# A four-layer graph network: destination bins in steps of two slots, layer 0 sums by half turn, a bilinear update in ten blocks, spread padding rows

## The reference, cut to what matters

```
edge_index = jnp.stack([src, dst])
h = jnp.maximum(_layernorm(x, axis=-1), 0.0)
x = x + _L0_gnn_ref(h, node_vec1, src, dst, edge_attr_4, edge_attr_12, ...)
...
# inside layer 0
ns = jax.ops.segment_sum(mid_s, edge_dst, num_segments=N) * inv
nv = jax.ops.segment_sum(mid_v, edge_dst, num_segments=N) * inv
...
# inside layer 2: a0, a1 are the summed messages, xs, xv the nodes
u0 = jnp.einsum('nu,nv,uvw->nw', xs, a0, Wu_ss) * INV64 + jnp.einsum('nui,nvi,uvw->nw', xv, a1, Wu_vv) * (INV_SQRT3 * INV32)
u1 = jnp.einsum('nu,nvi,uvw->nwi', xs, a1, Wu_sv) * INV_SQRT2048 + jnp.einsum('nui,nv,uvw->nwi', xv, a0, Wu_vs) * INV_SQRT2048
u0 = u0 + xs @ Lu_s * INV8
u1 = u1 + jnp.einsum('nui,uw->nwi', xv, Lu_v) * INV_SQRT32
```

## Time and profile before

| | us |
|---|---|
| median of the runs | 14562.09 |
| all runs | 14611.6, 14537.42, 14562.09 |
| profiled execution, its own time | 14520.14 |
| its span | 14518.4 |
| granted TensorE clock, mean | 0.899 |

### The profile page before, as it was taken

The page is one execution under the profiler, slowest core; times in us unless marked ns, Lnnn a source line. Parts: engine busy times, 40 slices in busy tenths (PEclk is TensorE's granted clock), DMA queues, the critical chain, the costliest instruction groups (busy, mean ns, idle before and its releaser), DMA issues. The chain is left out here.

```text
span 14518.4 us, 298687 instructions
## 1 busy us (share of the span) xinstructions
PE 11751.5 (81%) x76172; PEld 8152.7 (56%) x76173; DVE 8626.0 (59%) x30542; ACT 5078.7 (35%) x15312; POOL 8651.1 (60%) x13301
## 2 busy tenths in 40 slices
PE   5445542888879999869996897799999999999998
PEld 1000000666645555336664797577777777777776
DVE  6455552899744443133332555677777777777776
ACT  0000000566512222111111000466666666666665
POOL 2777775676657676137775000466666666666665
PEclk9999999999979898655555898799999999999998
DMA  3101110333433335324448774000000000000001
GB/s 139 27 24 27 27 26 11 69 69 68 57 61 74 69 72 65 23 56 82 82 82 55 119 116 72 17 18 18 18 17 18 18 18 17 18 18 18 17 18 19
DMA packets 1123580, 666.64 MB, mean 46 GB/s; under 512 B 711710, under 2 KB 1045491, under 8 KB 1117786
## 3 DMA queue, kind: packets, MB, share of 16 engines
q0 software_dynamic: 257120, 382.51, 15.3%
q1 hardware_dynamic: 850410, 235.44, 9.4%
q10 hardware_dynamic: 15568, 43.25, 0.8%
HBM read 574.19 MB, written 86.47 MB: 46 GB/s over the span
## 5 line engine op out<-in xcount | busy, mean ns | idle before, releaser
L1099 POOL DMA_INDIRECT l2s_node_rows<-node_table,l2s_edge_rows x1216 | 1154.3, 949 | 871.0 <-DMA l2s_edge_rows<-rows_by_src 486.7
L1099 POOL DMA_INDIRECT l1s_node_rows<-node_table,l1s_edge_rows x1216 | 1256.4, 1033 | 648.5 <-issue 320.9
L1184 PE MATMUL l1s_p_outer<-l1s_edge_by_node,l1s_node_rows 128*32 128x64 f32 (+2 forms) x14592 | 1242.6, 274 | 130.6 <-DMA l1s_node_rows<-node_table,l1s_edge_rows 96.0
L448 PE MATMUL rank<-onehot,lower_h 128*128 128x418 f16 x812 | 429.6, 529 | 1021.9 <-DVE onehot L424 958.7
L1184 PE MATMUL l2s_p_outer<-l2s_edge_by_node,l2s_node_rows 128*64 128x40 f32 (+1 forms) x4864 | 1038.8, 345 | 247.9 <-DMA l2s_node_rows<-node_table,l2s_edge_rows 245.7
L731 POOL DMA_INDIRECT l_source_rows<-node_table,l_edge_rows x928 | 949.8, 1023 | 436.6 <-issue 271.7
L1184 PEld LDWEIGHTS l2s_p_outer<-l2s_edge_by_node,l2s_node_rows 128*64 128x64 f32 (+1 forms) x4864 | 839.0, 233 | 638.4 <-issue 412.3
L1184 PEld LDWEIGHTS l1s_p_outer<-l1s_edge_by_node,l1s_node_rows 128*32 128x32 f32 (+2 forms) x14592 | 768.5, 132 | 685.5 <-issue 509.9
L461 POOL DMA_INDIRECT rows_by_src<-row_s,pos_i x812 | 839.7, 1034 | 494.3 <-issue 494.3
L1855 POOL DMA_INDIRECT l_source_rows<-node_table,l_edge_rows x914 | 899.0, 984 | 318.6 <-issue 246.4
L1883 POOL TENSOR_TENSOR l_logits_kept<-l_logits,l_empty_row 128x8 f32<-128x8 f32 x456 | 432.0, 947 | 979.4 <-DVE l_logits L2164 979.4
(11 more groups left out here) (495 smaller groups left out, 32003.1 us busy)
## 6 DMA issues: line engine op xcount, KB each, us to landing
l_xv_by<-h_turned_l SPq DMA_DIRECT2D x300, 128.0 KB
l_source_rows<-node_table,l_edge_rows POOLq DMA_INDIRECT x1842
l_xs_by<-h_turned_l SPq DMA_DIRECT2D x100, 256.0 KB
l_a_by<-sums_turned_l SPq DMA_DIRECT2D x100, 256.0 KB
rows_by_src<-zero_rows ACTq DMA_DIRECT2D x23, 1024.0 KB
l1s_edge_rows<-rows_by_src SPq DMA_DIRECT2D x304, 76.0 KB
l2s_edge_rows<-rows_by_src SPq DMA_DIRECT2D x304, 76.0 KB
l1s_node_rows<-node_table,l1s_edge_rows POOLq DMA_INDIRECT x1216
```

Of the source, the lines that this page charges most:

```text
L448: nc.tensor.matmul(rank[:, b, 0:BINS], K["lower_h"][:, :], onehot[:, b, :], start=True, stop=False)
L1099: pool.indirect_dma_start(xg[q][:, s, :], None, table, bass.IndirectOffsetOnAxis(ap=pay[q][:, s, S_DST:S_DST + 1].bitcast(U32), axis=0)).t ...
L1184: ins = nc.tensor.matmul(p_o[rows, j % RING, col:col + n], xg[q][:, s, lhs], rhs(eh[q % RING][:, s, :, :]), start=True, stop=True, skip_gr ...
```

## The change

**Destination bins are padded to PAIR = 2 slots.** The bound on slots becomes 856 (214 quads, 216 turns of layer 0; 428 pairs, 432 turns of layer 3), and the sort's shift uses 2 x 128.

```
-QUADS_D = -(-((E + BINS_D * (QUAD * P - 1)) // (QUAD * P)) // 2) * 2
-SLOTS_D = QUADS_D * QUAD
+PAIR = 2
+SLOTS_D = -(-((E + BINS_D * (PAIR * P - 1)) // (PAIR * P)) // 2) * QUAD
+QUADS_D = SLOTS_D // QUAD
```

```
-                        pe.wait_ge(added, q + 1)
-                        for s in range(QUAD):
-                            ins = nc.tensor.matmul(p_sum[:, k, 0:MW], hot[k][:, s, :], msg[k][:, s, :], start=s == 0, stop=s == QUAD - 1)
-                        ins.then_inc(summed, 1)
+                        for h in range(HALVES):
+                            pe.wait_ge(added, HALVES * q + (h + 1))
+                            for s in range(PAIR):
+                                ins = nc.tensor.matmul(p_sum[:, h, 0:MW], hot[k][:, PAIR * h + s, :], msg[k][:, PAIR * h + s, :], start=s == 0, stop=s == PAIR - 1)
+                            ins.then_inc(summed, 1)
...
+                        for h in range(HALVES):
+                            dve.reg_load([bin_regs[h]], bins[0:1, bass.ds(q * QUAD + PAIR * h, 1)])
+                        for h in range(HALVES):
+                            b = dve.snap(bin_regs[h], min_val=0, max_val=NB - 1)
+                            dve.wait_ge(summed, HALVES * q + (h + 1))
+                            dve.wait_ge(added, HALVES * q + (h + 2))
+                            to = acc[:, bass.ds(b, 1), :].rearrange("p o f -> p (o f)")
+                            nc.vector.tensor_tensor(to, to, p_sum[:, h, 0:MW], ALU.add).then_inc(added, 1)
```

```
             @block.scalar
                 act.wait_ge(cleared, 1)
+                act.wait_ge(keys_in, 96)
                 n = 0
...
-                        act.dma_start(flat[:, at:at + w], zero[:, 0:w]).then_inc(zeros_written, 16)
+                        act.dma_start(flat[:, at:at + w], pad[:, :, :].rearrange("p r w -> p (r w)")[:, 0:w]).then_inc(zeros_written, 16)
```

```
+            on_pool = [len(members) == 3 and n == 2 for _, members, _ in groups for n, _ in enumerate(members)]
...
+                    eng.wait_ge(used, t * OPS + (OPS + used_for[m]))
+                    x, y = of(k)
+                    (nc.gpsimd if pool else nc.vector).tensor_tensor(prod[m % BUFS][:, :, :], x, free(y, [0, KB], [1, W]), ALU.mult).then_inc(made, 1)
...
+                                for j, w in enumerate(weights):
+                                    if kind == "v":
+                                        for i in range(3):
+                                            ins = mm(thirds[i], w, prod[(m0 + i) % BUFS][:, j, :], start=False, ...)
+                                    else:
+                                        ins = mm(halves[1 - j % 2], w, prod[m0 % BUFS][:, j, :], start=s_seen == 0, stop=stop)
```

```
+                    nc.vector.tensor_tensor(xb[:, 0:CS], turn[k][:, 0:CS], xb[:, 0:CS], ALU.add).then_inc(x_added, 1)
+                    nc.vector.tensor_tensor(xb[:, CS:D], turn[k][:, P:P + 3 * CV], xb[:, CS:D], ALU.add)
+                    dve.wait_ge(x_added, b + 2)
+                    nc.vector.tensor_tensor(xb[:, 0:CS], turn[k][:, CS:2 * CS], xb[:, 0:CS], ALU.add).then_inc(x_done, 1)
```

More of the change, by code:

```diff
@@ L321, in _ @@
                 nc.vector.memset(junk[:, 2, 0:1], 0.0).then_inc(keys_ready, 1)
+            @block.gpsimd
+            def _(pool):
+                nc.gpsimd.iota(spread_i[:, :], pattern=[[N // PAD_R, PAD_R]], base=0, channel_multiplier=0).then_inc(spread, 1)
             @block.tensor
@@ new lines, in stage_layer2, with upto @@
+            first_of = [sum(len(g[1]) for g in groups[:n]) for n in range(len(groups))]
+            def upto(m, pool):
+                return sum(1 for q in on_pool[:m] if q == pool)
+            had = [m - BUFS if m >= BUFS else max(x for x in range(OPS) if x % BUFS == m % BUFS) - OPS for m in range(OPS)]
+            freed = {}
+            for n, (_, members, _) in enumerate(groups):
+                for m in range(first_of[n], first_of[n] + len(members)):
+                    freed[m] = first_of[n] + len(members)
@@ L1551, in _ @@
                     v.after()
[L1552 to L1561 removed]
+                    dve.sem_inc(made_d, DVE_OPS)
@@ L1563, in _ @@
+                    with dve.Fori(0, T // 2) as tt:
+                        for k in range(2):
+                            products(dve, 2 * tt + k, k, False, made_d)
+                @block.gpsimd
+                def _(pool):
+                    pool.sem_inc(made_p, POOL_OPS)
+                    with pool.Fori(0, T // 2) as tt:
+                        for k in range(2):
+                            products(pool, 2 * tt + k, k, True, made_p)
                 @block.tensor
                 def _(pe):
-                    pe.sem_inc(used, STEPS)
```

302 lines of the change are left out of this document (188 added, 114 removed).

## The result

| | before | changed |
|---|---|---|
| median, us | 14586.85 (4 runs, 14537.42 to 14614.98) | 13978.19 (4 runs, 13953.48 to 14006.55) |
| profiled execution, its own time | 14520.14 | 14000.75 |
| its span | 14518.4 | 13999.0 |
| granted TensorE clock, mean | 0.899 | 0.880 |

The ratio is 0.9587, with a 95% interval from 0.9548 to 0.9626. The forecast was 13,945 in a range of 13,650 to 14,120. The medians lie 609 us apart, the profiled executions 519: the profiled execution before lies 67 us under its median, the changed one's 23 us above. The ratio is as the runs gave it; the quotient of the two medians is 0.9583.

A forecast was written before the change was run, and what follows sets the result against it. The bound was sought per stage: DVE in layer 0's loop, PE in the bilinear update. Terms -274 + 145 - 50 - 59 - 88 - 12 - 257 - 22 = -617 gave 13,903 us profiled, 13,945 median; range 13,650 to 14,120.

The forecast's parts named there:

- Fewer turns of layer 3: Layer 3's loop: 24 fewer turns of a pair at 11.43 us each, nothing inside a turn changed, -274 us.
- Layer 0: Layer 0's loop: 12 fewer turns, each remaining one with an uncovered extra register load and add, +145; tail -12 us.
- Order of the first transfers: Start: clearing writes wait for the destination keys, which arrive some 50 us sooner, by 35 to 40 us, -50 us.
- Spread padding: Node sums: last gathers run at the middles' rate; layer 1 -59, layer 2 -88, layer 0's last turns -12 us.
- Rival C: Node sums' tails: spreading the padding does nothing, +159, giving 14,104 us; chance 0.10.
- The update: Bilinear update in ten blocks: DVE's and POOL's products exclude each other and add to 67 us a block, -257 us.
- Rival B: Bilinear update: POOL's products lie beside DVE's, a block is DVE's 42.3 us, 248 less, 13,697 us; chance 0.13.
- PE side by side: Bilinear update: three 32-column or two 64-column matmuls at once, PE about 35 us a block, under 67.
- D: Bilinear update: side by side matmuls run serially at full clock, 88 us a block, +206, 14,151 us; chance 0.04.
- E: Bilinear update: serial matmuls with TensorE granted 0.50, 176 us a block, +1083, 15,028 us; chance 0.03.
- Stage back: Stage back: two buffers and half the pieces, at the copies' and adds' pace of 1.1 us, -22 us.

The follow-up runs named there:

- four-slot run: Destination bins padded to four slots again, with one sum and one add per layer 0 turn, against the changed kernel: 14044.84 us, ratio 0.9635 to the kernel before.
- zero-padding run: Changed kernel with padding rows all holding node 0 again: 14088.91 us against the unedited rerun's 13952.96, ratio 0.968 to the kernel before.
- Two runs: Changed kernel, clearing writes not waiting for the keys: 13933.71 us; kernel before with its tile of zeros set twice: 14475.1 us against 14545.99.
- its second: Profile of the changed kernel run again with no edit: median 13952.96 us, ratio 0.9612 to the kernel before.
- the ten with spread padding: Ten kernels with spread padding, run where the kernel before takes some 14,570 us; their layer 1 took 2172 to 2302 us.
- the PSUM run: Changed kernel with ACT copying DVE's factor into PSUM for 28 of its 30 products a block: 13700.42 us, ratio 0.9423 to the kernel before.

## Why the prediction was right, point by point

- **Fewer turns of layer 3 (-274).** Measured -286: 24 turns of 11.40, and 0.03 us less per turn. The four-slot run gives 269 by itself.
- **Layer 0 (+145, with -12 of the tail).** Measured +154.5 in all, +171 from the first add to the last and -17 after it. The mechanism was right: DVE closes the turn and both additions stand bare. Each was slightly under-sized. The second register load took 0.49 us (0.90 less 0.41) and not 0.41, and the turn 7.01 instead of 6.89, 26 us. From the last add to layer 1's first gather it is 17 us shorter than before (157.3 against 174.1), where 12 were forecast for the padding; the zero-padding run gives 5 of them to it, and the rest is open.
- **Order of the first transfers (-50).** Measured -64. The size was about right. That the keys suffered from writes begun ahead of their load was right as well; that it took the wait for the keys to mend it was wrong. Two runs show that a clearing tile ready some 2 us later does it alone, all but 3 to 5 us. I also had the keys arrive at 35 to 40 us, and they came before 24.
- **Spread padding (-59, -88, -12).** Layer 2: -83 measured, where the forecast for the piece was -79 with 9 us of later products in it (the first product waited 19.1 us for its loads, 20.6 forecast), and 73 by the run with zeros. Layer 1's -59 isn't shown. The changed kernel's first profile is 64 us up and its second 66 down; the ten with spread padding have a mean of 2237 us against 2238 before. The step that failed was to take layer 1's clock as fixed: the row it rested on, 54 gathers in the last full window, stands at a granted clock of 0.66 with PE 98% busy, and the changed kernel has 48 at 0.62 with spread padding. A DMA share of 0.89 stands there as well, so the padding may have its part. Rival C is out by layer 2: padding of node 0 makes 73 us there and 5 in layer 0.
- **The update (-257).** From the first product to the end of its stage 653 us against 675 forecast. DVE's product came every 1.406 us alone (1.41 taken). POOL's takes 2.9 us, where I took 3.1 from two narrow rows; the estimate of 2.8 from the Trainium skill's GPSIMD Engine Reference, section 3.1, was the nearer one. The block is 65 us, 67 forecast, and near a sum of the two engines' products, but not by the step that I took. DVE's 300 products fill 618 us with the hold and 421 without it (the PSUM run), so each POOL product holds DVE up by 197 / 80 = 2.5 us and not by its full 2.9, or the 3.1 taken; the 31 us of DVE's waits for PE come on top. A block is 42.1 + 19.7 + 3.1 = 65 us. That the two come so near to full exclusion is partly luck: with four POOL products a block the hold is 1.4 us each and the waits are more than twice as long. Rival B (no blocking) would have been right with DVE's factor in PSUM: 443 us against the 424 that it gave.
- **PE side by side (rivals D and E).** 24 records in 2.35 us refute both. The clock in the stage fell to 0.79, as it was feared, without PE becoming the bound.
- **Stage back (-22).** 50 to 29 us. Layer 3's preparation was 11 us shorter without a forecast.
- **The sum.** -617 against -519 in the profiled executions and -609 in the medians. That the medians fit so well is partly chance: layer 1's clock moves either by up to 65 us. Of the 33 us by which the time lies over 13,945, 25 come from the median before, 14562.09 at the time of the forecast and 14586.85 now.

## What to carry to other kernels

Before a share of elementwise work goes to a second engine, look for a pair of rows in which the two overlap, and read whether the longer one ends with the other. Here the share cost 112 us against none at all, and with one operand moved to PSUM the same share gained 90. A register load in a loop is paid in full where its engine closes the turn (one load in place of two took 0.40 us off the turn), and one load of four values costs little more than one of one value (0.50 us of idle time against 0.41). And look at the order in which the first large transfers are issued across queues: two microseconds of order were worth sixty.

## What the runs showed of the hardware that was not expected

- An issue on SP's queue was held 44.58 us when 1 MB writes from ACT's queue had begun 1.2 us before it, and 2.2 us when they began 1 us after it. The keys then were there within 8 us of the last issue, with the writes beside them.
- Under the mutual hold, POOL is the one that starves: a product of 2.9 us took up to 19.4 us while DVE's came back to back, and DVE's never took over 4.22.
- In layer 1's node sums PE is busy 98.7 to 100% of the windows shown and yet the clock is granted 1.00 in some and 0.56 to 0.62 in others. The two profiles of one kernel have the falls at other places.
